# Cross-attention on one core: weights turned by output slices and Wk loaded in quarters; attention of two late units spread over steps

## What is computed

```python
q = (queries @ Wq.T + bq).reshape(B, Nq, HEADS, D_K).transpose(0, 2, 1, 3)   # B = 8, Nq = 224
k = (keys @ Wk.T + bk).reshape(B, Nk, HEADS, D_K).transpose(0, 2, 1, 3)      # Nk = 750
v = (values @ Wv.T + bv).reshape(B, Nk, HEADS, D_K).transpose(0, 2, 1, 3)
att = softmax(einsum('bhqd,bhkd->bhqk', q, k) / sqrt(D_K))
out = einsum('bhqk,bhkd->bhqd', att, v).transpose(0, 2, 1, 3).reshape(B, Nq, HEADS * D_K) @ Wo.T + bo
out = queries + out
out = (out - mean) / sqrt(var + 1e-05) * gamma + beta
```

## Time and profile before

| engine | busy us | share |
|---|---|---|
| TensorE products | 645.8 | 95% |
| VectorE | 476.1 | 70% |
| ScalarE | 331.9 | 49% |
| GpSimd | 455.4 | 67% |

### The profile page before, as it was taken

How to read it: one execution, slowest core, us unless ns; L and a number is a source line. 1 busy time by engine, 2 the same in 40 slices (tenths; PEclk the granted TensorE clock), 3 DMA queues, 4 the chain that set the end, 5 groups by cost and what they waited for, 6 DMA issues and landing times.

```text
span 676.4 us, 15102 instructions
## 1 busy us (share of the span) xinstructions
PE 645.8 (95%) x5433; PEld 448.0 (66%) x5433; DVE 476.1 (70%) x680; ACT 331.9 (49%) x657; POOL 455.4 (67%) x458
## 2 busy tenths in 40 slices
PE   6999999999999999999999999999999999997893
PEld 5756666766767666776767667776677767664451
DVE  4657667787767786777767787677867877664875
ACT  4514545455555455554455545555455545543470
POOL 9302765866967588576857679575867759675962
PEclk9999999999999999999999999999999999998798
DMA  9383323232232223332233322322233201330010
GB/s 289 113 210 89 82 75 75 53 95 51 74 98 70 65 74 86 85 71 88 56 82 84 88 74 56 95 70 67 83 81 90 51 1 41 93 80 23 1 56 28
DMA packets 39514, 53.08 MB, mean 78 GB/s; under 512 B 13388, under 2 KB 25688, under 8 KB 39448
## 3 DMA queue, kind: packets, MB, share of 16 engines
q1 hardware_dynamic: 39448, 52.16, 28.9%
HBM read 24.52 MB, written 3.67 MB: 42 GB/s over the span
## 4 chain that ended last, share of the span: by engine, by line
PE 86%; DVE 7%; issue 3%; POOL 2%; DMA 1%; ACT 1%; SPq 0%; POOLq 0%; DVEq 0%; ACTq 0%
PE ps_task L472 38%; PE ps_scores L483 11%; PE ps_task L521 11%; PE ps_scoresT L507 10%; PE ps_task L436 6%; PE ps_scores L472 3%; PE ps_task L446 2%; DVE top L741 2%; PE ps_task L547 2%; DMA ctx_in<-in_ctx 1%; DVE y L715 1%; PE ps_scoresT L492 1%; PE ps_task L450 1%; POOL pair_sums L850 1%; DVE parts L703 1%
## 5 line engine op out<-in xcount | busy, mean ns | idle before, releaser
L741 DVE TENSOR_REDUCE top<-ps_scores 112x1 f32<-112x750 f32 x256 | 235.4, 926 | 120.7 <-PE ps_scores L483 120.3
L850 POOL TENSOR_TENSOR pair_sums<-probsT 125x672 f32<-125x672 f32 x122 | 198.8, 1629 | 174.8 <-ACT probsT L642 169.7
L642 ACT ACTIVATE probsT<-ps_scoresT 125x448 f32<-125x448 f32 x384 | 189.0, 548 | 111.2 <-PE ps_scoresT L507 107.8
L483 PE MATMUL ps_scores<-stacks 96*112 96x512 f16 (+1 forms) x512 | 125.6, 327 | 4.3 <-DVE top L741 3.0
L472 PE MATMUL ps_task<-wvT,ctxT 128*125 128x512 f16 x552 | 127.2, 380 | 0.7 <-DVE ctxT L705 0.6
L472 PE MATMUL ps_task<-ctxT,wkT 128*128 128x375 f16 x696 | 120.7, 323 | 0.1
L507 PE MATMUL ps_scoresT<-stacks 100*125 100x224 f16 x768 | 116.9, 265 | 2.3 <-ACT probsT L642 0.4
L507 PEld LDWEIGHTS ps_scoresT<-stacks 100*125 100x125 f16 x768 | 81.6, 136 | 35.2 <-ACT probsT L642 18.4
L472 PEld LDWEIGHTS ps_task<-wvT,ctxT 128*125 128x125 f16 x552 | 73.0, 136 | 38.9 <-DVE ctxT L705 0.9
L472 PEld LDWEIGHTS ps_task<-ctxT,wkT 128*128 128x128 f16 x696 | 67.6, 97 | 36.8 <-DVE v L708 0.5
L855 POOL TENSOR_TENSOR head_sums<-pair_sums 125x224 f32<-125x224 f32 x122 | 84.5, 693 | 10.4
(11 more groups left out here) (96 smaller groups left out, 599.2 us busy)
## 6 DMA issues: line engine op xcount, KB each, us to landing
stacks<-parts SPq DMA_DIRECT2D x256, 60.9 KB, 2.0
ctx_in<-in_ctx SPq DMA_DIRECT2D x16, 672.0 KB
stacks<-parts SPq DMA_DIRECT2D x128, 46.9 KB, 2.0
x_in<-in_x SPq DMA_DIRECT2D x8, 448.0 KB, 3.7
resid<-in_x SPq DMA_DIRECT2D x8, 448.0 KB, 3.8
out_y<-y SPq DMA_DIRECT2D x16, 224.0 KB, 2.3
stacks<-parts SPq DMA_DIRECT2D x128, 14.0 KB, 1.8
ctx_in<-in_ctx SPq DMA_DIRECT2D x16, 78.0 KB
```

Source lines behind the costliest of these rows:

```text
L483: last = nc.tensor.matmul(ps_scores[0:QP, s % RING, keys], stacks[0:STACK_ROWS, g, h, NK + QP * q:NK + QP * q + QP], stacks[0:STACK_ROWS, ...
L642: nc.scalar.activation(probsT[0:KP, g % 2, h, 2 * j:2 * j + 2, :].rearrange("p k q -> p (k q)"), ps_scoresT[0:KP, piece % 2, 0:2 * NQ], AC ...
L741: nc.vector.tensor_reduce(top[0:QP, g % 2, HG * q + h:HG * q + h + 1], ps_scores[0:QP, s % RING, 0:NK], AX.X, ALU.max).then_inc(top_ready, 1)
L850: nc.gpsimd.tensor_tensor(pair_sums[0:KP], probsT[0:KP, g % 2, h, 0:3, :], probsT[0:KP, g % 2, h, 3:6, :], ALU.add).then_inc(pair_sums_rea ...
```

## The change

Weights are turned by slices of 128 output rows: `W`(w, f) turns the four column tiles of row tile f, so K and Q of unit g need slice g alone, V still all four. Wk is loaded in four DMAs of 128 rows with a semaphore each. SP's order becomes: first quarter of Wk, first half of ctx, x, biases, the other three quarters, second half of ctx, Wq, Wv, Wo. The prologue's tasks are reordered with it, K(0,0) and K(1,0) ahead of the second half of ctx, and after the first task TensorE does four more products of the identity. Units 28 and 29 are attended one key tile a step (steps 2 to 7 after the old visit's unit began), summed in step 7, and copied a unit later; unit 29's copy to low fall in steps 0 to 5 of the tail. From step 16 of the last batch both output projections use bank 0 of `ps_task`, the units bank 1. In the tail the projections no longer wait for a save two steps back, and times gamma and plus beta of half 0 move from steps 22 and 23 to 24 and 25, behind the rstd of half 1.

```diff
--- before.py
+++ after.py
@@ -38,6 +38,7 @@
     RING = 2
     PIECES = 3 * HG
     WARM_UP = 8
+    KEEP_UP = 4
     MAX_SCALE = 1024.0
     NU = B * UNITS
     VECTOR_HEADS = (HG * (NU - 1) - 2, HG * (NU - 1) - 1)
@@ -67,7 +68,11 @@
 
     STAGES = {**{("attend", k): (2, VISIT) for k in range(KT)}, "sum_keys": (2, VISIT), "copy": (2, 2), ("invert", 0): (2, 3),
               ("invert", 1): (2, 4), "scale": (2, 5), "high": (2, 6), "low": (2, 7)}
-    TAIL = {NU - 2: {**{("attend", k): max(k, 1) for k in range(KT)}, "sum_keys": 5, "copy": 6, ("invert", 0): 7, ("invert", 1): 8,
+    SPREAD = {**{("attend", k): (2, 2 + k) for k in range(KT)}, "sum_keys": (2, 7), "copy": (3, 0), ("invert", 0): (3, 1),
+              ("invert", 1): (3, 2), "scale": (3, 3), "high": (3, 4), "low": (3, 5)}
+    SPREAD_FROM = NU - UNITS
+    TAIL = {NU - 3: {"copy": 0, ("invert", 0): 1, ("invert", 1): 2, "scale": 3, "high": 4, "low": 5},
+            NU - 2: {**{("attend", k): max(k, 1) for k in range(KT)}, "sum_keys": 5, "copy": 6, ("invert", 0): 7, ("invert", 1): 8,
                      "scale": 9, "high": 10, "low": 10},
             NU - 1: {"copy": 11, ("invert", 0): 12, ("invert", 1): 13, "scale": 14, "high": 15, "low": 16}}
     HIGH_STEP, LOW_STEP = STAGES["high"][1], STAGES["low"][1]
@@ -77,12 +82,22 @@
     assert UNIT + LOW_STEP < O_STEPS[0] and O_STEPS[1] < 2 * UNIT + HIGH_STEP
     STEP_OF = {t: s for s, t in {**OWN, **NEXT, **OUTPUT}.items()}
     SPLIT_KINDS = ("ctxT", "xT", "K", "Q", "W")
-    prologue = ([("xT", 0), ("xT", 1)] + [("ctxT", i) for i in range(3)] + [("W", "k", k) for k in range(DT)]
-                + [("ctxT", i) for i in range(3, KT)] + [("K", 0, 0), ("W", "q", 0), ("W", "q", 1), ("K", 0, 1),
-                   ("W", "q", 2), ("W", "q", 3), ("K", 1, 0), ("Q", 0), ("W", "v", 0), ("W", "v", 1), ("W", "v", 2), ("W", "v", 3),
-                   ("K", 1, 1), ("W", "o", 0), ("W", "o", 1), ("W", "o", 2), ("W", "o", 3), ("Q", 1), ("K", 2, 0), ("V", 0), ("K", 3, 0), ("V", 1), ("V", 2)])
+    prologue = [("W", "k", 0)] + [("ctxT", i) for i in range(3)] + [("xT", 0), ("xT", 1), ("W", "k", 1), ("W", "k", 2), ("K", 0, 0),
+                ("K", 1, 0), ("W", "k", 3), ("ctxT", 3), ("ctxT", 4), ("ctxT", 5), ("K", 2, 0), ("W", "q", 0), ("W", "q", 1),
+                ("K", 0, 1), ("Q", 0), ("W", "q", 2), ("W", "q", 3), ("K", 1, 1), ("W", "v", 0), ("W", "v", 1), ("Q", 1),
+                ("W", "v", 2), ("W", "v", 3), ("K", 3, 0), ("W", "o", 0), ("V", 0), ("W", "o", 1), ("W", "o", 2), ("V", 1),
+                ("W", "o", 3), ("V", 2)]
     PRO = len(prologue)
     PRO_BIASES = prologue.index(("K", 0, 0))
+
+    def prologue_inputs(t):
+
+        if t[0] not in "KQV":
+            return []
+        found = [("W", "v", f) for f in range(DT)] if t[0] == "V" else [("W", t[0].lower(), t[1])]
+        if t[0] == "Q":
+            return found + [("xT", 0), ("xT", 1)]
+        return found + ([("ctxT", t[1])] if t[0] == "V" else [("ctxT", i) for i in range(3 * t[2], 3 * t[2] + 3)])
 
     def tasks_of(b):
 
@@ -205,7 +220,7 @@
 
 
         ctx_loaded, x_loaded = [sem(f"ctx_loaded{i}") for i in range(2)], sem("x_loaded")
-        w_loaded = {w: sem(f"w{w}_loaded") for w in "qkvo"}
+        w_loaded = {w: [sem(f"w{w}{f}_loaded") for f in range(DT if w == "k" else 1)] for w in "qkvo"}
         bias_loaded, rows_loaded, bias_turned = sem("bias_loaded"), sem("rows_loaded"), sem("bias_turned")
         resid_loaded = sem("resid_loaded")
         stacked = [[sem(f"stacked{g}_{h}") for h in range(HG)] for g in range(UNITS)]
@@ -256,9 +271,14 @@
 
             if isinstance(b, int) and b == B:
                 return [(u, u % UNITS) for u in TAIL if TAIL[u].get(stage) == s]
-            back, at = STAGES[stage]
-            u = unit_before(b, s // UNIT, back)
-            return [(u, (s // UNIT - back) % UNITS)] if s % UNIT == at and u is not None else []
+            found = []
+            for stages in (STAGES, SPREAD):
+                back, at = stages[stage]
+                u = unit_before(b, s // UNIT, back)
+                spread = isinstance(u, int) and u >= SPREAD_FROM
+                if s % UNIT == at and u is not None and spread == (stages is SPREAD):
+                    found.append((u, (s // UNIT - back) % UNITS))
+            return found
 
         def head_and_tiles(u, piece):
 
@@ -273,7 +293,11 @@
 
         def task_bank(b, s):
 
-            return ps_task[:, O_STEPS.index(s) if isinstance(b, int) and b == B else s % TASK_BANKS]
+            if isinstance(b, int) and b == B:
+                return ps_task[:, O_STEPS.index(s)]
+            if isinstance(b, int) and b == LAST and s >= 2 * UNIT:
+                return ps_task[:, 1 - VISIT_BANK]
+            return ps_task[:, s % TASK_BANKS]
 
         def to_save(b, s):
 
@@ -287,6 +311,8 @@
 
             if isinstance(b, int) and b == B:
                 return NU - 2
+            if isinstance(b, int) and b == LAST and s >= 2 * UNIT:
+                return None
             at = s - TASK_BANKS
             tasks = tasks_of(b)
             while at >= 0 and at not in tasks and at % UNIT != VISIT:
@@ -308,7 +334,7 @@
                 i = t[1]
                 return xT[:, part, :, QP * i:QP * i + QP], bank[:, 0:DT * QP].rearrange("p (k t) -> p k t", k=DT), None
             if kind == "W":
-                return wT[t[1]][:, part, t[2], :], bank[:, :], None
+                return wT[t[1]][:, part, :, P * t[2]:P * t[2] + P], bank[:, :].rearrange("p (k f) -> p k f", k=DT), None
             g = t[1]
             if kind == "K":
                 return parts[:, g, part, KH * t[2]:KH * t[2] + KH], bank[:, 0:KH], bias16["k"][:, g:g + 1]
@@ -349,14 +375,19 @@
                 sp.dma_start(dram(out, b).rearrange("(q p) d -> p q d", p=QP)[:, q], y[0:QP, q]).then_inc(stored, DMA)
 
             def load_w(w, W):
-                sp.dma_start(w_in[:, "qkvo".index(w)], W.rearrange("(t p) d -> p t d", p=P)).then_inc(w_loaded[w], DMA)
-
+                sp.dma_start(w_in[:, "qkvo".index(w)], W.rearrange("(t p) d -> p t d", p=P)).then_inc(w_loaded[w][0], DMA)
+
+            def load_wk_rows(f):
+                sp.dma_start(w_in[:, "qkvo".index("k"), f], Wk[P * f:P * f + P]).then_inc(w_loaded["k"][f], DMA)
+
+            load_wk_rows(0)
+            load_ctx(0, 0)
             load_x(0)
-            load_ctx(0, 0)
-            load_w("k", Wk)
-            load_ctx(0, 1)
             for i, v in enumerate((bk, bq, bv)):
                 sp.dma_start(bias_rows[DT * i:DT * i + DT], v.rearrange("(t p) -> t p", p=P)).then_inc(bias_loaded, DMA)
+            for f in range(1, DT):
+                load_wk_rows(f)
+            load_ctx(0, 1)
             load_w("q", Wq)
             load_w("v", Wv)
             load_w("o", Wo)
@@ -449,9 +480,10 @@
                     for k in range(DT):
                         last = nc.tensor.transpose(bank[:, QP * k:QP * k + QP], x_in[0:QP, t[1], P * k:P * k + P], ident[0:QP, 0:QP])
                 elif kind == "W":
-                    pe.wait_ge(w_loaded[t[1]], DMA)
-                    for f in range(DT):
-                        last = nc.tensor.transpose(bank[:, P * f:P * f + P], w_in[:, "qkvo".index(t[1]), f, P * t[2]:P * t[2] + P], ident[:])
+                    if t[1] == "k" or t[2] == 0:
+                        pe.wait_ge(w_loaded[t[1]][t[2]], DMA)
+                    for k in range(DT):
+                        last = nc.tensor.transpose(bank[:, P * k:P * k + P], w_in[:, "qkvo".index(t[1]), t[2], P * k:P * k + P], ident[:])
                 elif kind == "O":
                     last = project_output(t[1], bank, range(UNITS), batch)
                 else:
@@ -513,6 +545,8 @@
 
                 if k == 0:
                     pe.wait_ge(probs_ready, PIECES * (u + 1))
+                    if isinstance(u, int) and u >= SPREAD_FROM:
+                        pe.wait_ge(attn_copied, u)
                 if g == 0 and k not in EARLY_V:
                     place = next(place for t, place, _ in iteration_tasks(batch).values() if t == ("V", k))
                     pe.wait_ge(task_saved, tasks_before(batch) + place + 1)
@@ -557,10 +591,12 @@
                 if n == PRO_BIASES:
                     pe.wait_ge(bias_loaded, 3 * DMA)
                     nc.tensor.transpose(ps_scoresT[:, 0, 0:3 * DT], bias_rows[:], ident[0:3 * DT, 0:3 * DT]).then_inc(bias_turned, 1)
-                if t[0] in "KQ":
-                    own = [("xT", 1)] if t[0] == "Q" else [("ctxT", 3 * t[2] + 2)]
-                    pe.wait_ge(task_saved, max(prologue.index(i) for i in own + [("W", t[0].lower(), DT - 1)]) + 1)
+                if t[0] in "KQV":
+                    pe.wait_ge(task_saved, max(prologue.index(i) for i in prologue_inputs(t)) + 1)
                 task(t, n, pro_banks[n % PRO_BANKS], 0)
+                if n == 0:
+                    for _ in range(KEEP_UP):
```

(5 more changed lines are left out.)

## The result

| | median us | runs | profiled run, us | span | mean granted clock |
|---|---|---|---|---|---|
| before | 679.52 | 678.57 to 680.62 | 678.81 | 676.4 | 0.988 |
| changed | 672.26 | 669.24 to 674.81 | 673.01 | 670.3 | 0.985 |

The ratio is 0.9885, with a 95% interval from 0.9862 to 0.9908: 7.3 us less by the medians, 5.8 us between the two profiled runs. The forecast was 8.5 us, that is 671.7 for the median. Its sum was nearly right, but two of its terms were not, in opposite directions.

What follows compares the result with a forecast made beforehand. TensorE, never free in the steady part, bounds the kernel, so savings at either end carry whole to the end. 2.3 + 7.0 - 0.9 + 0.1 = 8.5 us off 680.19 gives 671.7; eight in ten runs 665.5 to 677.0.

Steps and rivals of the forecast that it cites:

- step (d): Last batch, steps 27 to 31: VectorE sets the pace, 7.8 us to 640.4; a lower clock may add 0.5.
- start: Prologue: Wk quarters and new load order cut TensorE's idle from 3.79 to 1.5 us; gain 2.3, ends 1.0 and 2.8.
- tail, to the last projections: Tail: unit 29's copy on ScalarE costs 0.5 us and its late high part more; loss 0.9, ends 0 and 2.
- last outputs: End of run: reordering gamma and beta gains 0.1 us, as VectorE and GpSimd block each other; 1.1 if nothing blocked.
- 6.9 - 5.4 = 1.5: Start: TensorE's remaining idle in us, from the first Wk slice's end to the first ctx half's landing.
- Part 2: Last batch's second half: spreading units 28 and 29 removes a 3.52 us wait; gain 7.0 us, ends 3 and 10.
- R4: Last batch, 7%: spreading leaves TensorE about 72% busy and at 1.2 GHz from step 18; 7.5 us slower, 687.7.
- step (c): Last batch: centring waits for GpSimd's late rstd and holds row maximum 26; TensorE stands 2.6 us from 630.1.
- +1, of which TensorE's queued work covers 0.6: Tail: unit 29's high part, 6.9 us after the turning, holds step 5's exponentials on ScalarE, due at 6.4.
- R2: Last batch and tail, 22%: the wait moves to GpSimd, its queue full to 644.0; gain only 4.5 us, 675.7.
- R1: Last batch and end, 20%: no standstill at step 27, blocks pass beside other work; gain 13.2 us, 667.0.
- R3: Start, 8%: x or the Wk quarters land late and the old 3.79 us stay; start 0, rest 6.2, 674.0.

Runs made afterwards that it cites:

- e8: The changed kernel without the four filler products of the identity at the start; one run, 668.32 us.
- e1: Only the start of the change, with the last batch and tail as in the kernel before; 676.71 us against 679.83, ratio 0.9955.
- e3: The changed kernel with ten more products of the identity behind step 26 of the last batch; 668.51 us, ratio 0.9849.
- e4: The changed kernel with the centring of output 1 moved from step 24 to 27 of the last batch on VectorE; 667.30 us, ratio 0.9820.
- e9b: The changed kernel run again with nothing edited; 671.18 us, ratio 0.9862.
- e7: The changed kernel with Wk in one load, first in SP's order, instead of quarters; one run, 671.62 us.
- e10b: The changed kernel with ten more products of the identity behind step 28 of the last batch; 675.29 us, ratio 0.9897.
- e11b: The changed kernel with times gamma and plus beta of half 0 back in steps 22 and 23, ahead of half 1's rstd; one run, 670.02 us.
- e5: e4 with GpSimd's times gamma and plus beta of batch 6 moved to steps 1 to 4 of the tail; 665.36 us against 680.31, ratio 0.9785.
- e2: The kernel before with only the last batch and tail parts of the change, the start as before; 676.10 us, ratio 0.9958.

## Why the prediction was right, and where not

The forecast for the median, 671.7 us, is 0.6 below the measured 672.26. Its mechanisms were right in the main; what it mis-sized most is the clock behind the standstill, step (d). That the sum came so near is in part luck: it had 0.5 us for a stretch at the low clock that lasted 13.6 us in one trace of this kernel and 3.4 in another, its runs lie anywhere from 669 to 675 us, and a start that gave more than forecast covers part of it. Against the profiled run, 673.01 for a forecast of 670.3, it is off by 2.7 us.

| step | forecast, us | profiled run | a run with the short low stretch (e8) |
|---|---|---|---|
| start | 2.3 | 3.1 | 2.9 |
| last batch, to the turning of 648.03 | 7.0 | 3.2 | 7.0 |
| tail, to the last projections | -0.9 | -0.5 | -0.4 |
| last outputs | 0.1 | 0.4 | 0.4 |
| sum (measured: of the spans) | 8.5 | 6.1 | 9.9 |

**The start** was too small by 0.8 us. Its mechanism was right: the first ctx half was used at 6.80 (6.9 forecast), K(0,0) begins at 10.10 (10.4), no load is waited for after that, and e1 carries it to the end. The term that failed is the idle, "6.9 - 5.4 = 1.5", and that nothing else was counted. In the profiled run the gap before ctx, fillers aside, is 6.80 - 5.51 = 1.29 us, which gives 2.5. The first tile began at 4.91, where the first one before began at 5.11: 0.2 more, which is no work of the change, since e1, e3, e4, e8 and e9b have 5.11 to 5.12 as well. And the same twelve tiles take 5.54 us in the new chain of waits, where they come nearly in one row, and took 5.92 in the old one, in three groups behind idle time: 0.4 more. In e8 the first slice ends later, at 6.03, and the idle is 0.99: 3.79 - 0.99 = 2.8, of 2.85 us gained. e7 shows which part bears it: the quarters, with the slices that make them useful. The forecast's 2.3 is near the low end of what the traces give (46.62 - 44.20 = 2.4 to 47.16 - 43.43 = 3.7).

**Part 2** was right step by step up to the standstill. Projection one ended and rstd of output 1 came within 0.3 us of the walk less the start's 3.1, step 23 ended 1.1 us later than walked, and the sums of unit 28 had no wait. The new standstill was forecast at 630.1 for 2.6 us, before the start's 2.3 to 3.1 us are taken off; it is there, 2.46 us, up to 629.36. The hold of centring by rstd and by a pair sum is there too. Step (d) failed in its clock term, 0.5 us. With the short low stretch (e8) it is about right, since the walk fits within 0.1 us; in the profiled run of the changed kernel it takes 3.8 us more (17.6 - 13.8). R4 had the mechanism, at a chance of 7%: the clock stays at 0.50 although TensorE is never idle. But it took TensorE's share of busy time for the cause and the whole half for its length. (The sum of R4 has a slip too: 10 - 2.3 is 7.7, not 7.5.) What the low stretch follows is the standstill that step (c) had itself found; the profiled runs of e3 and e4, which close it in two ways, keep 1.00 there. It is not the only thing that a fall can follow, as e10b shows at 610 us. To charge 0.5 us for it was to let VectorE's pace, 1.5 us a step, cover most of it; a step at 1.2 GHz took 2.45 us, not the 2.1 worked out (scores 0.80, pieces 0.75, attend 0.91, from the start of one to that of the next), and the stretch lasted all five steps.

**The tail.** The loss from the turning to the last projections is 0.5 us, and 0.35 in e8; TensorE waits there for unit 29's copy, 0.18 us in the profiled run and 0.40 in e8. The other term, "+1, of which TensorE's queued work covers 0.6", did not come in the profiled run: VectorE began its two head sums at 638.56, 3.2 us before the turning and not with it, so the high part was early, and ScalarE waited for TensorE before the exponentials of step 5:

```profile
648.20 0.98 ACT L678 ACTIVATE probsT<-ps_scoresT 125x448 f32<-125x448 f32 x2 [0.45 <-PE ps_scoresT L539]
```

In e8 VectorE begins them at 637.96, 0.2 us before the turning, and ScalarE does stand 1.37 us for VectorE's scaling ahead of that high part, as forecast; but TensorE has no wait from it, so its queued work covers all of it.

**Last outputs.** 0.4 in all (13.46 - 13.08), of which e11b gives the reorder 0.26; the 0.12 left go with the other edits. 0.1 was forecast, 1.1 without the block. The block is what was forecast, with gamma at 1.56 us.

**The rivals.** R2, GpSimd's queue as the next bound, appears only once the clock is cured (e4, 1.39 us). R1's 13.2 us is reached and passed by e5, 680.31 - 665.36 = 15.0 us, with one centring and four operations of GpSimd moved. R3 is out: in the changed kernel no load is waited for after 6.80, in e1 only x, 0.26 us at 8.81.

## What to carry to other kernels

Before a wait that is taken off an engine is counted as gain, walk the queues of the engines that take over, and look for an instruction whose wait holds others behind it; here one centring of 0.5 us of work cost a standstill of 2.5 us and up to 5 us of clock behind it (17.6 us from turning to turning, 12.7 in e3). A standstill of TensorE of that size is not priced by its own length. Where rstd or the like comes from a slow queue, put its consumer some steps later: by the ratios, 0.9885 to 0.9820, e4 gained 4.4 us, where the whole second half of the change (e2) gives 2.9.
